# PSUM copies of the transposes moved to ScalarE, first x tile loaded in four pieces: pre-norm linear layer on eight cores

## The reference, cut to what matters

```python
def _layernorm(x, axis=-1, eps=1e-5):
    m = jnp.mean(x, axis=axis, keepdims=True)
    v = jnp.var(x, axis=axis, keepdims=True)
    return (x - m) / jnp.sqrt(v + eps)
...
    x = L0_attn_x                                   # (1, 8192, 4096) f32
    x = x + _L0_attn_ref(_layernorm(x, axis=-1))
    # ffn: w_b = aa * tanh(kk * weight);  y = x @ w_b.T;  return y + bias
    x = x + _L0_ffn_ref(_layernorm(x, axis=-1), L0_ffn_weight, L0_ffn_bias, L0_ffn_kk, L0_ffn_aa)
```

## Time and profile before

| what | us |
|---|---|
| median of the runs (2) | 621.84 |
| lowest, highest | 619.42, 624.27 |
| the profiled execution, its own time | 621.2 |
| its span (core 1, the slowest) | 619.6 |
| spans of cores 0 to 7 | 606.7, 619.6, 619.4, 606.7, 604.1, 611.6, 610.6, 616.0 |
| PE, PEld, DVE, ACT, POOL busy on core 1 | 500.6, 232.2, 172.3, 200.8, 83.6 |

### The profile page before, as it was taken

How to read it: one execution, slowest core, us unless ns; L and a number is a source line. 1 busy time by engine, 2 the same in 40 slices (tenths; PEclk the granted TensorE clock), 3 DMA queues, 4 the chain that set the end, 5 groups by cost and what they waited for, 6 DMA issues and landing times.

```text
span 619.6 us, 7134 instructions; the slowest of 8 cores (604.1 to 619.6 us)
## 1 busy us (share of the span) xinstructions
PE 500.6 (81%) x2379; PEld 232.2 (37%) x2379; DVE 172.3 (28%) x368; ACT 200.8 (32%) x196; POOL 83.6 (13%) x118
## 2 busy tenths in 40 slices
PE   3034567653766999999979996999899999999993
PEld 3021233331333444444434442444344444444441
DVE  1450366754766210212020301220302032022120
ACT  0256566653233154005500552035106302520000
POOL 0001000100000212111211120102203020211111
PEclk9566687678677999999999999999999999999997
DMA  7959777199812689898999999989989978998742
GB/s 213 290 206 273 222 257 231 43 270 305 201 37 52 146 282 260 230 152 284 242 258 128 302 282 252 214 214 300 261 203 282 282 209 246 298 239 192 160 109 68
DMA packets 47699, 134.72 MB, mean 217 GB/s; under 512 B 5680, under 2 KB 5680, under 8 KB 46640
## 3 DMA queue, kind: packets, MB, share of 16 engines
q0 software_dynamic: 16416, 43.00, 34.6%
q1 hardware_dynamic: 20016, 50.37, 25.5%
q10 hardware_dynamic: 11232, 40.90, 21.4%
HBM read 117.47 MB, written 16.78 MB: 217 GB/s over the span
## 4 chain that ended last, share of the span: by engine, by line
DMA 40%; PE 31%; ACT 11%; DVE 5%; issue 5%; ACTq 3%; POOL 2%; DVEq 1%; SPq 1%; POOLq 0%
PE ps_acc L321 28%; DMA wring<-w2d 20%; DMA outs<-biasrow 11%; ACT wp L231 6%; DMA rb<-x 6%; DMA xs<-x 4%; PE ps_tr L295 2%; DVE stats L161 2%; ACT h2T L251 2%; POOL outs L355 1%; ACTq L234 1%; ACT h2b L245 1%; ACTq L222 1%; ACT L240 1%; DVE outs L149 1%
## 5 line engine op out<-in xcount | busy, mean ns | idle before, releaser
L321 PE MATMUL ps_acc<-wp,h2T 128*128 128x512 bf16 x2048 | 461.9, 389 | 30.5 <-ACT wp L231 19.3
L321 PEld LDWEIGHTS ps_acc<-wp,h2T 128*128 128x128 bf16 x2048 | 203.7, 100 | 285.1 <-issue 55.9
L231 ACT ACTIVATE wp<-wring,kk_sb 128x1024 bf16<-128x1024 f32 x128 | 147.0, 1148 | 244.9 <-DMA wring<-w2d 190.9
L149 DVE SCALAR_TENSOR_TENSOR outs<-rb,s1a,ps_acc 128x512 f32<-128x512 f32 x64 | 47.7, 746 | 333.3 <-DMA rb<-x 234.8
L355 POOL DMA_DIRECT2D outs<-biasrow x64 | 56.6, 1072 | 268.2 <-DVE outs L153 254.8
L295 PE MATMUL ps_tr<-ident_sb,h2b 128*128 128x128 bf16 x256 | 33.2, 292 | 52.0 <-DVE h2b L197 37.5
L337 POOL DMA_DIRECT2D wring<-w2d x50 | 28.5, 603 | 261.6 <-ACT wp L231 247.6
L295 PEld LDWEIGHTS ps_tr<-ident_sb,h2b 128*128 128x128 bf16 x256 | 22.5, 127 | 64.7 <-issue 64.7
L161 DVE BATCH_NORM_STATS2 stats<-xs 128x6 f32<-128x512 f32 x64 | 38.7, 677 | 20.8 <-DMA xs<-x 20.8
L153 DVE TENSOR_SCALAR outs<-outs,b1a 128x512 f32<-128x512 f32 x64 | 32.3, 505 | 5.7 <-issue 0.9
L203 DVE CAST h2T<-ps_tr 128x512 bf16<-128x512 f32 x32 | 22.1, 692 | 37.1 <-PE ps_tr L295 37.1
(11 more groups left out here) (21 smaller groups left out, 30.7 us busy)
## 6 DMA issues: line engine op xcount, KB each, us to landing
wring<-w2d ACTq DMA_DIRECT2D x78, 512.0 KB, 7.8
wring<-w2d POOLq DMA_DIRECT2D x50, 512.0 KB, 6.8
xs<-x SPq DMA_DIRECT2D x8, 2048.0 KB, 12.4
rb<-x SPq DMA_DIRECT2D x64, 256.0 KB, 8.8
outs<-biasrow POOLq DMA_DIRECT2D x64, 256.0 KB, 9.5
y<-outs SPq DMA_DIRECT2D x64, 256.0 KB, 7.1
ident_sb<-ident SPq DMA_DIRECT2D x1, 32.0 KB, 3.4
kk_sb<-kk SPq DMA_DIRECT2D x1, 0.5 KB, 2.0
```

Source lines behind the costliest of these rows:

```text
L149: vector.scalar_tensor_tensor(outs[g % 4][:, :], rbb[g % 4][:, :], s1a[:, t:t + 1], ps_acc[g % 4][:, :], ALU.mult, ALU.add)
L231: scalar.activation(wp[ot % 2][:, jop * WPC:(jop + 1) * WPC], wr[:, sl * WPC:(sl + 1) * WPC], AF.Tanh, bias=0.0, scale=kk[:, :]).then_inc( ...
L321: mm = tensor.matmul(ps_acc[g % 4][:, :], h2T[:, t * D + ic * 128: t * D + (ic + 1) * 128], wp[ot % 2][:, ic * 512:(ic + 1) * 512], start= ...
```

## The change

Three edits:

1. ACT copies all eight parts of each tile's transposes, the odd ones in place of DVE. `s_evTo` goes; PE waits on `s_evT` alone. The two `ps_tr` banks stay.
2. x tile 0 is loaded by four DMAs of 1024 columns, each with a semaphore (`s_x0`); DVE's statistics wait for one piece at a time, ACT and POOL wait for the last. `ident` is loaded ahead of `kk` and `aa`.
3. The counts of `s_xin[0]` drop by one load; POOL's helper is written inline, with the same DMAs in the same order.

```diff
     @block.sync
     def _(sync):
+        sync.dma_start(ident[:, :], id_h[:, :]).then_inc(s_const, 16)
         sync.dma_start(kk[:, :], kk_h[:, :]).then_inc(s_const, 16)
         sync.dma_start(aa[:, :], aa_h[:, :]).then_inc(s_const, 16)
-        sync.dma_start(ident[:, :], id_h[:, :]).then_inc(s_const, 16)
-        sync.dma_start(xs[0][:, :], x_h[0:128, :]).then_inc(s_xin[0], 16)
+        for j in range(4):
+            sync.dma_start(xs[0][:, 1024 * j:1024 * (j + 1)],
+                           x_h[0:128, 1024 * j:1024 * (j + 1)]).then_inc(s_x0[j], 16)
         sync.dma_start(xs[1][:, :], x_h[128:256, :]).then_inc(s_xin[1], 16)
...
         for t in range(NT):
             p = t % 2
-            vector.wait_ge(s_xin[p], 16 * (t // 2 + 1))
+            if t == 0:
+                pass
+            elif p == 1:
+                vector.wait_ge(s_xin[1], 16 * ((t + 1) // 2))
+            else:
+                vector.wait_ge(s_xin[0], 16 * (t // 2))
             for j in range(8):
+                if t == 0 and j % 2 == 0:
+                    vector.wait_ge(s_x0[j // 2], 16)
                 vector.bn_stats(stats[:, 48 * p + 6 * j:48 * p + 6 * j + 6],
                                 xs[p][:, 512 * j:512 * (j + 1)])
...
-            for k in range(1, 8, 2):
-                vector.wait_ge(s_trT, 8 * t + k + 1)
-                vector.tensor_copy(h2T[:, t * D + k * 512: t * D + (k + 1) * 512],
-                                   ps_tr[1][:, :]).then_inc(s_evTo, 1)
             for g in evac_after_tile[t]:
                 emit_evac(g)
...
-            for k in range(0, 8, 2):
+            for k in range(8):
                 scalar.wait_ge(s_trT, 8 * t + k + 1)
                 scalar.copy(h2T[:, t * D + k * 512: t * D + (k + 1) * 512],
-                            ps_tr[0][:, :]).then_inc(s_evT, 1)
+                            ps_tr[k % 2][:, :]).then_inc(s_evT, 1)
 
         scalar.wait_ge(s_const, 48)
-        scalar.wait_ge(s_xin[0], 16)
+        scalar.wait_ge(s_x0[3], 16)
...
                 if trg >= 2:
-                    u = trg - 2
-                    tensor.wait_ge(s_evT if u % 2 == 0 else s_evTo, u // 2 + 1)
+                    tensor.wait_ge(s_evT, trg - 1)
...
         gpsimd.wait_ge(s_const, 48)
-        gpsimd.wait_ge(s_xin[0], 16)
+        gpsimd.wait_ge(s_x0[3], 16)
```

More of the change, by code:

```diff
@@ L64, in build_nc @@
     s_xin = [es.enter_context(sem(f"s_xin{i}")) for i in range(2)]
+    s_x0 = [es.enter_context(sem(f"s_x0{i}")) for i in range(4)]
     s_rb = [es.enter_context(sem(f"s_rb{i}")) for i in range(4)]
@@ L72, in build_nc @@
     s_evT = es.enter_context(sem("s_evT"))
-    s_evTo = es.enter_context(sem("s_evTo"))
     s_trT = es.enter_context(sem("s_trT"))
@@ L309, in _ @@
             if ot > 0:
-                tensor.wait_ge(s_evT, 4 * (t + 1))
-                tensor.wait_ge(s_evTo, 4 * (t + 1))
+                tensor.wait_ge(s_evT, 8 * (t + 1))
             if g >= 4:
@@ L317, in _ @@
                 if ot == 0 and ic % 4 == 0:
-                    k = ic // 4
-                    tensor.wait_ge(s_evT if k % 2 == 0 else s_evTo,
-                                   4 * t + k // 2 + 1)
+                    tensor.wait_ge(s_evT, 8 * t + ic // 4 + 1)
                 mm = tensor.matmul(ps_acc[g % 4][:, :],
@@ L343, in evens @@
                 w = ot * NW + j
-                if w % NWS >= 3:
-                    issue_piece(w)
+                sl = w % NWS
+                if sl < 3:
+                    continue
+                if w >= NWS:
+                    gpsimd.wait_ge(s_wp, w - NWS + 1)
+                gpsimd.dma_start(wr[:, sl * WPC:(sl + 1) * WPC],
+                                 w_h[ot * 128:(ot + 1) * 128,
+                                     j * WPC:(j + 1) * WPC]).then_inc(s_wl[sl], 16)
         evens(0)
```

## The result

| | before | with the change |
|---|---|---|
| median us (runs) | 622.86 (11) | 615.28 (12) |
| lowest to highest us | 619.42 to 626.26 | 606.21 to 620.5 |
| ratio to before, 95% interval | | 0.983 (0.978 to 0.988) |
| the profiled execution, its time | 621.2 | 607.66 |
| its slowest core, span | core 1, 619.6 | core 3, 606.1 |

The account below looks back on a forecast made before the run. A chain of small steps bounds the tile phase, PE the main phase. Delays of 2.6 and 0.5 us, outweighed in tiles 5 to 7, start group 7 5.8 us earlier: 621.84 - 5.8 = 616.0, range 611 to 620 (8 in 10: 610 to 622.5).

Parts of the forecast that it names:

- The bound and the rigid main phase: From 199 us on: PE-bound, DMA close behind, untouched by the edits; gain is group 7's earlier start, 5.8 us.
- The second rival: Main phase: DMA-bound, so an earlier PE only waits longer; time stays at 620 to 623 us; chance 0.20.
- Start, +0.5: Tile 0: faster statistics hidden behind the fifth weight piece; smaller DMA rows cost 0.5 us, bounds 0 to 3.3.
- Tiles 0 to 4, +2.6 by x tile 5: Tiles 0 to 3: ACT's extra trailing copies make x tile 5 be asked for 2.6 us later.
- Tiles 5 to 7: Late tile phase: earlier DVE statistics remove PE's waits of 3.94 and 4.13 us; group 7 at 193.3 against 199.14.
- The evacuation on one engine: ACT copying all parts: two banks' round trip stays 1.41 us, eight parts 5.6 us, one trailing copy adds 0.62.
- The start that gains: Tile 0: the 3.6 us of faster statistics come through, time 612.4 us; chance 0.06.
- x tile 5 late by its bias addition: Bias addition at 121.23: takes 18.3 us, x tile 5 lands 8.1 later still, time 624 us; chance 0.06.
- the point of decision: Landing of x tile 5: the late-load rival decides once it is over 5.8 us beyond the reckoned 3.1.
- Turns of one engine: Transposes and copies alternate at 1.40 us a part, each block 5.6 longer, time 655 us; chance 0.02.

Follow-up runs that it names:

- e1: The kernel before with ACT making all copies, x tile 0 still in one load: median 613.68 us against 623.36, ratio 0.982.
- e8: The change, with ACT making all copies only in tiles 5 to 7, x tile 5 loaded early, no PE waits for first weights: 597.78 us against 617.12.
- e4: The kernel before with ACT making all copies in tiles 5 to 7 only, shared with DVE in tiles 0 to 4: ratio 0.978.
- e2: The kernel before with x tile 0 in four pieces and ident first, copies still shared: median 624.63 us against 623.36, ratio 1.003.
- e3: As e1, but DVE waits before its evacuation until ACT has made the tile's last copy: 624.88 us against 623.36 before, ratio 1.004.

## Why the prediction was right

**The time.** 616.0 forecast, 615.28 measured; 5.8 us of gain forecast, 7.6 between the medians, 7.8 in the start of group 7, 10.6 by the ratio. The path and its order were right. That the medians lie 0.7 us from the forecast is partly luck: the tile phase gave more than the sum has, and the main phase was 3.0 us shorter in the profile (416.0 to 413.0), of which e1 shows only 0.5. The terms, on the mean of the cores:

- *The bound and the rigid main phase.* Right within some microseconds. From group 7 to the end it takes 412.9 to 418.0 us in all thirteen profiles of the table, while group 7 starts anywhere from 174.5 to 198.6. The second rival (the main phase takes it back) is out: e8 moved group 7 by 21.4 us and the mean span by 24.2 (611.8 less 587.6).
- *Start, +0.5.* Right in kind (nothing gained), undersized: the weights are asked for 1.1 us later and the first transposes come 1.3 later. I had bounded it by packet rates, 0 to 3.3. The scaled tile was ready 2.4 us sooner (25.7 to 23.3) and not 3.6, since the last piece lands 1.1 later than the whole tile did. One more step was off: three more DMAs on SyncE were put at 0.47 us each, but the four pieces took 3.01 us to issue, and x tile 1 went out at 5.48 for 2.90, 2.6 us later and not 1.4. The trace of before had a warning: its four residual loads took 3.13 us to issue.
- *Tiles 0 to 4, +2.6 by x tile 5.* The statistics of tile 5 start 3.8 later, for 3.1 with the start's share. e4 measured the copies' part alone, 3.1. But the sum held because two errors met: the step between neighbouring tiles grew less than 0.62 (by 0.5 from group 1 to 2, where it went from 18.75 to 19.24 us, and by 0.2 in the two steps behind), and group 1 came 1.9 later.
- *Tiles 5 to 7.* The mechanism was right and its size too small: from group 5 to group 7 I had 27.1 us, it took 24.6. The blocks of transposes, put at 5.4, took 4.6 and 4.8 on the mean (4.46 in the rows above), and groups 5 and 6 with no idle time behind them 8.0 and 7.2 (the starts of the next transposes), for 8.39 and 7.85. That is the term that was mis-sized: it saves 8.9 us in my sum and 11.4 in the profiles. I had left the warmer clock out of the sum and in the range. The page of the Trainium skill that bears on it is TensorE: Matmul & The Clock Gate, section Why this matters for your kernels, which asks that PE has no long idle gaps between bursts of matmuls. By that rule the trace agrees: granted clock 0.96 for 0.78 where the waits of 4 us went.
- *The evacuation on one engine.* The rule of TensorEngine Tiling (Array Packing), PSUM Bottleneck, in the Trainium skill, to use both engines for the evacuation, did not decide here: the pair's round trip stayed 1.40 us. But it is not wrong either. In tiles 0 to 4, where DVE has nothing better to do, sharing is better by 2.9 us (e4), and in tiles 5 and 6 one engine is better, because the other has the statistics of the next tile to carry.
- *The rivals.* The start that gains: out by e2. x tile 5 late by its bias addition: it took 7.46 us on core 3, and 7.1 to 10.5 over the cores for 7.4 to 10.2 before, so the point of decision (5.8 us more) was never near. Turns of one engine: out by the 1.40; its price was also added up wrong, as 36 us above 621.84 is 658 and not 655.

## What to carry to other kernels

When work is moved from one engine to another, ask what the first engine does next and who waits for it. Here four copies of 0.7 us a tile were worth over 10 us (group 7 at 188.1 in e1, 198.6 with DVE held in e3). It is not their own time but their place: they kept DVE until the transposes were done, and behind them stood the statistics of the next tile; on tiles where nothing waited behind them the same move cost 3. A stretch hidden behind a DMA stays hidden whatever is done to it, and when the cover is removed the next limit may be the loads and not the step that was sped up.

## What the runs showed of the hardware that I had not expected

- A load of 2 MB cut in four column pieces, rows of 4 KB for 16 KB, left a core with less moved by 14 us on the mean (2.72 MB for 2.95), and in an uneven way: half of the cores kept 3.0 MB, the others fell to 2.4. All kernels with the pieces have 2.7 MB, all without them 2.9 to 3.0. Issuing the four took SyncE 3.01 us; the one load before took 0.43.
- Two PSUM banks emptied by one engine run at 0.70 us a part when PE has been idle before the transposes, and at 0.60 (4.69 us for eight, less 0.58 and over seven steps: 0.59) when a group of matmuls stood directly before (tile 6 of core 3); the copy of 0.58 us is then the limit.
